# Second attention of a four-layer kernel: a batch's eight gathers issued one by one instead of in two rows of four

## What is computed

```python
x = _layernorm(x + _L0_attn_ref(x, ...))   # 16 heads of 64, banded mask, softmax
x = _layernorm(x + _L0_ffn_ref(x, ...))    # 16 experts, each token takes the best 4
x = _layernorm(x + _L1_attn_ref(x, ...))   # 16 heads of 8, softmax, LoRA projections
x = _layernorm(x + _L1_ffn_ref(x, ...))    # gated scan over the 16 batches, then tanh
```

```python
sel = jnp.take_along_axis(exp_out, topi[..., None], axis=2)
fused = jnp.sum(w[..., None] * sel, axis=2)
```

## Time and profile before

| what | us |
|---|---|
| median of 3 runs | 1430.63 (1427.74 to 1431.56) |
| span of the profiled execution, from its first to its last instruction | 1445.1 |
| TensorE busy in it | 1272.4 (88%) |
| VectorE busy | 1014.5 (70%) |
| ScalarE busy | 931.4 (64%) |
| GpSimd busy | 770.7 (53%) |

### The profile page before, as it was taken

How to read it: one execution, slowest core, us unless ns; L and a number is a source line. 1 busy time by engine, 2 the same in 40 slices (tenths; PEclk the granted TensorE clock), 3 DMA queues, 4 the chain that set the end, 5 groups by cost and what they waited for, 6 DMA issues and landing times.

```text
span 1445.1 us, 36685 instructions
## 1 busy us (share of the span) xinstructions
PE 1272.4 (88%) x9756; PEld 971.6 (67%) x9756; DVE 1014.5 (70%) x3763; ACT 931.4 (64%) x2825; POOL 770.7 (53%) x981
## 2 busy tenths in 40 slices
PE   7999999999999999984899998996787788788973
PEld 3777776777777777764899998993455455455652
DVE  2677777777777777775677776766787677678835
ACT  5878777777777778772465665653565555556644
POOL 1557777777777777775222121235466666664132
PEclk9999999999999999997899999997899989999997
DMA  9612222221112222221222223222323223222102
GB/s 340 206 60 74 73 73 73 73 73 54 47 51 72 69 71 71 73 74 58 62 71 82 77 82 90 81 79 65 80 58 78 67 53 85 58 61 64 36 1 59
DMA packets 149016, 110.98 MB, mean 77 GB/s; under 512 B 12833, under 2 KB 137249, under 8 KB 148770
## 3 DMA queue, kind: packets, MB, share of 16 engines
q1 hardware_dynamic: 139842, 92.45, 22.0%
q0 software_dynamic: 8192, 16.79, 4.1%
q10 hardware_dynamic: 864, 0.39, 0.1%
HBM read 47.27 MB, written 61.93 MB: 76 GB/s over the span
## 4 chain that ended last, share of the span: by engine, by line
PE 60%; DVE 10%; issue 8%; ACT 7%; another core or an unknown queue 4%; DMA 3%; SPq 3%; DVEq 3%; ACTq 1%; POOL 0%; POOLq 0%
PE psum L911 9%; PE psum L922 8%; PE psum L798 6%; PE psum L835 6%; PE psum L853 5%; PE psum L746 4%; PE psum L815 3%; PE psum L753 3%; PE psum L947 3%; PE psum L747 3%; ACT wall L1183 2%; PE psum L935 2%; PE psum L1018 2%; ACT P L1153 2%
## 5 line engine op out<-in xcount | busy, mean ns | idle before, releaser
L554 POOL TENSOR_SCALAR P<-P,rinv 128x192 f32<-128x192 f32 (+1 forms) x384 | 308.5, 816 | 158.7 <-DVE rinv L1335 151.7
L1153 ACT ACTIVATE P<-shifted,least 128x192 f32<-128x192 f32 (+1 forms) x512 | 240.2, 470 | 100.6 <-DVE least L1321 99.1
L1175 ACT ACTIVATE hid<-psum,wA 128x128 f32<-128x128 f32 x576 | 164.4, 368 | 123.8 <-PE psum L911 120.2
L1512 DVE TENSOR_REDUCE mx<-psum 128x2 f32<-128x512 f32 x256 | 165.2, 687 | 66.4 <-PE psum L1018 42.3
L1321 DVE CUSTOM_DVE_ANT_0 shifted<-psum,band 128x192 f32<-128x192 f32 (+1 forms) x512 | 168.9, 385 | 27.5 <-PE psum L798 27.2
L598 POOL DMA_INDIRECT yk<-xs,posc x128 | 125.6, 981 | 107.4 <-DVE wA L1473 57.6
L1183 ACT ACTIVATE wall<-psum 128x1024 f32<-128x1024 f32 x128 | 130.8, 1022 | 65.7 <-PE psum L935 47.5
L911 PE MATMUL psum<-xgT,wA 128*128 128x128 f32 x1152 | 156.0, 279 | 2.0 <-ACT hid L1175 1.4
L922 PE MATMUL psum<-wB,hid 128*128 128x128 f32 x1152 | 152.6, 276 | 0.0
L911 PEld LDWEIGHTS psum<-xgT,wA 128*128 128x128 f32 x1152 | 143.3, 195 | 3.2 <-ACT hid L1175 1.8
L835 PEld LDWEIGHTS psum<-ident,P 128*128 128x128 f32 x1024 | 117.6, 141 | 35.8 <-issue 29.4
(11 more groups left out here) (261 smaller groups left out, 2537.0 us busy)
## 6 DMA issues: line engine op xcount, KB each, us to landing
xs<-zrow SPq DMA_DIRECT2D x34, 1024.0 KB
xg<-xs SPq DMA_DIRECT2D x144, 64.0 KB, 1.8
xs<-yrow SPq DMA_DIRECT2D x144, 64.0 KB
wall<-in_wall SPq DMA_DIRECT2D x1, 8232.0 KB, 36.3
qkd<-parts SPq DMA_DIRECT2D x64, 96.0 KB
kst<-qkd SPq DMA_DIRECT2D x22, 128.0 KB
qst<-qkd SPq DMA_DIRECT2D x22, 128.0 KB
wall<-qkd SPq DMA_DIRECT2D x20, 128.0 KB
```

Of the source, the lines that this page charges most:

```text
L554: g.tensor_scalar(x, x, rinv[:, par, n:n + 1], None, ALU.mult).then_inc(s["pn_ready"], 1)
L1153: last = sc.activation(P[:, par, it, h, 0:w], shifted[:, par, it, h, 0:w], ACT.Exp, scale=-1.0, bias=least[:, par, n:n + 1], accum_out=row ...
L1175: sc.activation(hid[:, n % 4, f, :], up(n, f), ACT.Gelu, bias=wA[:, n % 4, F + f:F + f + 1]).then_inc(s["hid_ready"], 1)
L1512: v.tensor_reduce(out=mx[:, :, h], in_=SB[(par + 1 + h) % 3].rearrange("q (i n) -> q i n", i=TT), axis=mybir.AxisListType.X, op=ALU.max).t ...
```

## The change

`outputs` no longer fetches half 0 in one row ahead of `keep` and half 1 in one row at its end. Of half 0 the first gather stays where it was, the second goes behind `keep`, the third behind `combine`, the fourth behind `new_state`. Of half 1 each gather waits for `max_done` first: gather k for 16 (b + 2) + 2 k, that is, for the row maxima of the first k steps of the next batch's loop. `need_alone` is a wait as an instruction of its own. The number of gathers, their sizes and their contents are the same.

```diff
             def outputs(b, par):
                 deviations(b)
-                fetch(b, par, 0)
+                fetch(b, par, 0, 0, 1)
                 keep(b)
+                fetch(b, par, 0, 1, 2)
                 combine(b, par)
+                fetch(b, par, 0, 2, 3)
                 new_state(b)
-                fetch(b, par, 1)
+                fetch(b, par, 0, 3, 4)
+                for k in range(TT * TOPK // 2):
+                    if has(b, 5):
+                        need_alone(pool, "max_done", H1 * (b + 2) + 2 * k)
+                    fetch(b, par, 1, k, k + 1)
```

## The result

The changed kernel takes 1434.47 us (median of 13 runs, 1428.97 to 1441.99), the kernel before, timed beside it, 1427.19 us (13 runs, 1424.44 to 1432.2). The ratio is 1.0052, 95% interval 1.0039 to 1.0065: slower by 7.3 us, more than the 0.3% that can be told from no change. The forecast was 1424 us and faster; the range, 1402 to 1440 us, holds the result.

The account below looks back on a forecast made before the run. It took close gathers holding back TensorE's completions in the second attention as the bound: 26.2 us gained, 20.7 lost, 1 gained in batches 0 to 2, 6.5 off the span, scaled to 6.4, giving 1424 us; range 1402 to 1440 us.

Parts of the forecast that it names:

- the hold: Second attention: while gathers follow each other within some 1.5 us, TensorE's completions reach the other engines late.
- Steps 6 to 7: Second attention, from ScalarE's exp of step 6 to that of step 7: 5.91 us per batch, forecast to become about 3.5.
- nothing moves: Rival, 1430 us, chance 0.10: the stall follows the number of gathers or the profiler's writing, so moving gathers saves nothing.
- The control from the expert stage: Expert stage before the second attention: lone gathers leave the tile pitch at 1.89 us; three close ones make a tile 3.74 us.
- Part 1: Half 0's gathers spread over 3 us apart, so their stall between exps 6 and 7 goes: gain 26.2 us.
- Part 2: Half 0's gathers 2 and 3 push later GpSimd work back 2.5 us; scan_done, comb_done and half 0's data stay covered.
- Part 3: The four max_done waits find their conditions met, cost 0 to 0.1 us each; half 1 still goes as a row, later.
- Part 4: Half 1's row starts at 12.1 us after exp 7, delaying exp 5 by 2.3 us in nine batches: loss 20.7 us.
- Slower, 1438 us: Rival, chance 0.21: the later row costs 20.7 us, spreading half 0 returns only 13, as lone gathers hold TensorE's completions.
- The later row escapes: Rival, 1407 us, chance 0.19: half 1's row starts 13.5 us or more after exp 7, so exp 5 is not delayed.
- The gather beside a VectorE operation: GpSimd gather beside VectorE's writing of parts: 4.7 us instead of 0.95 by the skill's ratio; the trace showed 1.54.

Follow-up runs that it names:

- recorded execution: The profiled execution of the kernel before from which the prediction was made, no edit: span 1445.1 us, against a median of 1427.19 us for its 13 runs.
- second look: The kernel before, unchanged, profiled again for a second trace: 1426.8 us, span 1425.0 us.
- third look: The kernel before, unchanged, profiled once more: 1423.0 us, span 1421.2 us.
- experiment 7: The changed kernel, with SP's loads of the stacked operands waiting until half 1's gathers have landed: ratio to before 1.0225.
- experiment 4: The kernel before with three idle GpSimd additions ahead of half 1's row, so only that row starts some 2.2 us later: ratio 1.0059.
- experiment 8: The kernel before with half 1's row earlier, its row-number copy moved behind combine and the xo addition behind the row: 1420.82 us against 1426.69, ratio 0.9965.
- experiment 9: The change without its four waits, half 1's row earlier by moving its row-number copy ahead and the xo addition behind: ratio to before 0.9995.

## Why the prediction was wrong

**What bounds the kernel: this failed first.** I took the hold of one recorded execution for a property of the kernel. Steps 6 to 7 at 5.91 us were that execution's; two more executions have 3.68 and 3.64 us (5.68 us is the recorded one's over the same batches, 1 to 11). The warning was in plain sight: the recorded span stood 14.5 us above the median of the runs. I scaled by 0.99 instead of asking whether the extra time was the very stall that I wanted to save. The rival "nothing moves", with a chance of 0.10, came nearest, by doubting the profiled execution. That the profiler's writing makes the hold isn't shown either, for two more profiled executions are without it.

The control from the expert stage doesn't hold. In the second look three gathers again go out 1.3 and 1.5 us apart, from 957.59, and a fourth at 962.06, and no tile beside them takes over 2.2 us; the third look and the changed kernel are the same. The tile of 3.74 us was the recorded execution's too. "A second within some 1.5 us starts the hold" was read from one execution and is contradicted by the others.

**Part 1, the gain of 26.2 us, is not there.** Against 3.53 us the kernel before has 3.68 - 3.53 = 0.15 us per batch to give, 11 x 0.15 = 1.7 us. (In that window of the earlier trace rows it is TensorE that is busy throughout, 3.53 of 3.53 us, and not ScalarE, with 3.07.) In the execution with the hold there was little of the stall that the kernel has otherwise: TensorE's waits for the loads between exp 0 and exp 1 were 8.3 us in the recorded execution and 33.1 us in the second look.

**Part 2 is the step that made the sign wrong.** It went through scan_done, comb_done and half 0's data, and left out the one consumer of what is pushed back furthest: ScalarE's weighing of half 1 in step 6. In the recorded execution half 1 lands at 16.5 us and exp 6, behind which it is wanted, starts at 20.6 us (the mean steps added up), which looks safe even 2.5 us later. In an execution without the hold it lands at 20.9 us, in batch 9 with 1.7 us to spare. The push of 2.5 us takes that in every second batch, and the landing itself grows from 4.5 to between 6.4 and 7.0 us, because the gather now starts in the midst of SP's loads. "SP's queue stays" was true and beside the point: what SP has under way decides how long GpSimd's gather takes, as experiment 7 shows. The Trainium skill states in "DMA: Bandwidth & Descriptors", section "Issuing engines are not separate DMA queues", that DMAs of all issuing engines run on the same 16 DMA engines and interleave. The traces agree that the two get in each other's way: the gather takes 2.4 to 2.6 us with the loads held back and up to 7.0 us beside them.

**Part 3 held in the main.** The waits cost nothing that the runs show (1.0004), and from batch 3 on half 1 went out as a row, 1.27 us apart. In the first row of the stage at least one wait wasn't met. The row began at 15.0 us in batch 9, not at 12, since the place before was 12.2 us without the hold and not 9.6. Half 0 was spread less than forecast: in every second batch its first two gathers are 2.3 us apart, not over 3, and the fourth starts 2.1 to 2.4 us ahead of half 1's row.

**Part 4, the loss of 20.7 us, failed with the hold.** Steps 4 to 5 take 4.02 us against 4.01 us. Nothing delays exp 5.

**The sum by what was measured.** Per batch, against the second look of before: steps 6 to 7 cost 5.00 - 3.68 = 1.32 us more, step 0 0.13 us more, steps 0 to 1 0.56 us less, all others together 0.15 us less; with the last digits kept that is 0.74 us, over 11 batches 8.1 us. The runs gave 7.3 us. That the range held the result is no merit: it reached up to 1440 us for the rival "slower", and the sum that gave 1424 us has both of its large terms from the hold.

**The rivals.** "Slower, 1438 us" had the right sign and the right place to look, steps 6 to 7 above 4.0 us, at 5.00 us. Its mechanism, lone gathers that hold TensorE, was wrong: experiment 4 has the loss with no gather of this stage spread. That its 7.7 us are close to the 7.3 us measured is luck, for neither of its two terms, 20.7 us lost and 13 us given back, is there. "The later row escapes" fails with the hold.

**The gather beside a VectorE operation.** The 4.7 us that the prediction estimates by a ratio has no ground in the traces. The gather of 1.54 us began at 1242.08, when 0.61 us of VectorE's L1579 were left, and took 0.59 us longer than the usual 0.95. In experiment 8's trace seven of half 1's gathers have some 0.39 us of the same operation left and take 0.38 us longer; one gather of the second look, at 1055.52, has 0.34 us left and takes 0.22 us longer. What is added in these traces is at most the rest of the operation and no multiple. Nor does the lock of the Trainium skill ("SBUF — State Buffer", section "SBUF: two separate sides") give a ratio: it keeps the one that came second waiting for the whole instruction of the other. The trace agrees with that reading, 0.59 us longer with 0.61 us left.

**Open.** Why the last gather is so late only in every second batch (18.8 us on average, in the others 16.1 to 16.6) was read from the trace and not tested: after a late exp 7 the next batch's time is counted from a later start, while GpSimd has gone on. What set off the hold is open too. What looks odd in experiment 9, that six of its nine last gathers start at 16.6 us on average and take 6.2 us, where in the kernel before those that start at 16.4 us take 4.5 us, has its answer in the traces. In five of these six batches SP's loads start 14.1 to 15.4 us behind exp 7, in the second and third look at the kernel before not until 15.5 us or later. So the six gathers start 1.1 to 1.7 us after the first of SP's loads, those of the kernel before from 0.8 us ahead of it to 0.3 us behind. The landing goes by the distance to the loads, not by the one to exp 7; the last section has all of them.

## What to carry to other kernels

When the order of issues on one engine changes, list for every transfer that gets later who reads it and how much it has to spare, in an execution whose time lies at the median of the runs; a stall in a profile that is 1% longer than the median of the runs may belong to that execution alone. A transfer that starts a little later can land much later when it slides into another queue's burst, so look at the data's landing and at the other queues, not at the issue. Here the useful move was the opposite one: half 1's row 2 us earlier, clear of the loads, took 0.35% off the time.

## What the runs showed of the hardware

The same indirect gather of 64 KB (half 1's last one, batches 3 to 11) lands 2.4 to 2.6 us after its start with SP's loads held back (experiment 7). In the twelve other recorded executions how long it takes goes with when it starts, counted from the first of SP's loads of the stacked operands nearest to it:

| starts | gathers | lands after its start |
|---|---|---|
| 1.2 to 2.5 us before the loads | 25 | 2.4 to 2.8 us |
| 0.7 to 0.9 us before | 7 | 2.8 to 3.8 us |
| with them, up to 0.4 us after | 39 | 4.0 to 5.0 us |
| 0.6 to 1.4 us after | 13 | 4.3 to 5.9 us |
| 1.6 to 1.9 us after | 9 | 4.3 to 6.7 us |
| 2.2 to 3.5 us after | 14 | 6.1 to 7.0 us |
| 4.2 us after | 1 | 6.0 us |

For the loads the same meeting shows as TensorE's waits, 33.1 and 31.9 us in the second and third look at the kernel before and 26.3 us with the row out of the way.

In one execution out of three of the kernel before, ScalarE and VectorE waited 78.4 us for releasers that the profile can't name (the seven "remote" rows of that view), many of them close behind rows of gathers; in the other two, in the changed kernel and in the nine variants, there is no such wait. What sets it off wasn't tested. The span of that execution was 20 us longer than the second look's, and the stall between exp 0 and exp 1 was 25 us shorter in it.
